# A causal mask of attention scores, added by two 64-row matmuls instead of one of 128 rows

## The chip, the cores and the metric

The kernel runs on one core of a Trainium2 chip. The metric is the device time of one execution in microseconds, as the median of several runs. TensorE is called PE here (PEld is its weight load), VectorE DVE, ScalarE ACT, GpSimd POOL, SyncE SP. All times are in microseconds unless marked ns.

## What is computed

The input x has 16 batches of 256 tokens with 128 features. Four layers follow each other, each with a layer norm in front and a residual behind: causal attention, a mixture of experts (8 experts, the best 2 for each token), a second attention without a mask, and the mixture of experts again. Only the first attention is touched by the change:

```python
B, T, D, H = (4, 256, 128, 16)      # x has 16 batches; HD = 8
q, k, v = proj(wq, bq), proj(wk, bk), proj(wv, bv)
scores = jnp.einsum('bhqd,bhkd->bhqk', q, k) * scale
mask = jnp.triu(jnp.full((t, t), NEG, jnp.float32), k=1)
attn = jax.nn.softmax(scores + mask, axis=-1)
out = jnp.einsum('bhqk,bhkd->bhqd', attn, v)
return out @ wo + bo
```

## The kernel before

Each attention layer is a pipeline over j = 0 to 19. In step j the engines work on several batches at once: the projections of batch j (P_), the values V and the scores S of batch j-2 (V_, S_), the transposed scores T of batch j-3 (T_), the output projection of batch j-4 (O_). Every engine has its own instruction stream, written out by hand (`pe_step`, `act_step`, `dve_step`, `pool_step`, `sp_step`), in which a loop over the 16 heads h carries the other work between the heads. The streams are tied by counting semaphores; `after(engine, semaphore, value)` is a wait.

q and k are split into three bf16 parts each, so that six products stand for one float32 product: 6 × 8 = 48 rows a head (50 for T, which carries minus the row maxima as two more rows). These rows of the even and odd heads stand in SBUF partitions 0 to 47 and 64 to 111 (`qst`, `kst`), so a score matmul uses one half of TensorE's 128 rows. For head h, with par = h % 2:

- S: scores of 128 queries by up to 256 keys, in row half par, in the PSUM bank `psS[par]`. S0 (queries 0 to 127, 128 columns) and S1 (queries 128 to 255, 256 columns) are both line 355. They are only needed for the row maxima.
- T: the transposed scores, in the other row half and the bank `psT[1 - par]`, T0 (256 columns) and T1 (128 columns), line 363. ACT takes their exponential into `pT` (line 553).
- The order of issue is S0, T0, S1, T1, then the mask of T (line 382, only in batches 14 and 15; in the others POOL clears the masked part of `pT`, line 790), then the mask of S (line 386). A mask is one matmul that multiplies the bf16 identity `identb` with a 128x128 triangle of -3e38 (`trib`, for T `tritb`) and adds it to the two diagonal blocks of the bank, 2 × 128 columns, over all 128 rows of the array.

DVE waits for the semaphore S, which the last of S's matmuls raises, and reduces the bank to row maxima (line 671). Before S0 of head h PE waits for the maximum of head h-2, before T0 for the exponential of head h-2. After the 16 heads of a half batch the maxima go through a transpose (line 342), ACT, DVE (line 633) and two DMAs to rows of `qst`.

Between the heads of a full step PE does, behind the mask of the head named: head 1 transposes of the maxima (line 342) and the last quarter of P·V (line 321); head 2 the transposes of x (269); heads 4 and 11 the output transposes (328); head 5 P·V, then the q and k projections (276, four matmuls a batch); heads 6 and 13 a transpose (333), at 13 behind P·V; heads 8 and 14 the output projection (337); head 9 P·V and the maxima (342); head 12 the values (426). Behind heads 0, 3, 7, 10 and 15 nothing stands, and the next head's S0 follows at once. P·V uses 32 weight columns a head and writes 32 output partitions.

DVE has, besides the maxima, the merge of the maxima of two halves (659), the layer norm of the next batch (583), normalising (641, 643), the residual (651), the values with their bias (705), and behind the maxima of heads 11 and 14 the residues of the bf16 split (627).

At the start POOL fills the constants (lines 1750 to 1758) and counts them on `s_const`; DVE waits for 6, after the layer norm of the first two batches, casts the identity to bf16 (line 1791) and permutes the weights (574, 576). PE waits in `pe_setup` for the permuted weights and for `s_const_dve` 2 and then makes the bias columns (line 254).

Of the kernel before, what the change touches and what calls it, by code (L numbers as in the profile page):

```python
# [8 lines left out]
BF16 = mybir.dt.bfloat16  # L9
I32 = mybir.dt.int32  # L10
ALU = mybir.AluOpType
ACT = mybir.ActivationFunctionType
AX_X = mybir.AxisListType.X

P = 128
B, T, D = 16, 256, 128
H, HD = 16, 8
NBLK = B * T // P
TERMS = 6
ROWS = TERMS * HD  # L20
E, HID = 8, 512
HB = HID // P
G = 2
# [8 lines left out]
OWN_A = 2 * (SIZE[0] + PART) + E - 1  # L32
CST_DESC, CST_TILE, CST_HEAD, CST_TRIU = 0, E, E + TILES, E + TILES + P
CST_COLS = CST_TRIU + P
FETCH = 3
EPS = 1e-5
NEG = -3.0e38
# [31 lines left out]
def build(nc, A, out):  # L69
    with ExitStack() as ctx:  # L70
        def sb(name, shape, dt=F32):
            return ctx.enter_context(nc.sbuf_tensor(name, shape, dt))

        def psum(name):
            return ctx.enter_context(nc.psum_tensor(name, [P, 512], F32))

        def sem(name):
            return ctx.enter_context(nc.semaphore(name))
# [5 lines left out]
        psS = [psum("psS0"), psum("psS1")]  # L84
        psT = [psum("psT0"), psum("psT1")]
# [5 lines left out]

        x = sb("x", [P, NBLK, D])
        cst = sb("cst", [P, CST_COLS])
# [2 lines left out]
        nwt = sb("nwt", [P, 3, NBLK])  # L96
        ident = sb("ident", [P, P])
        identb = sb("identb", [P, P], BF16)
        trib = sb("trib", [P, P], BF16)
        tritb = sb("tritb", [P, P], BF16)  # L100
        ones_row = sb("ones_row", [1, T])
# [24 lines left out]
        half = sb("half", [1, 2, H])  # L126
# [63 lines left out]
        s_const = sem("s_const")  # L190
        s_const_dve = sem("s_const_dve")
# [57 lines left out]
        def pe_setup(pe, L):  # L249
            s = L.s  # L250
            pe.wait_ge(s["wp"], 4)
            pe.wait_ge(s_const_dve, 2)
            for o in range(2):
                last = nc.tensor.matmul(psM[:, o:o + 1], L.b_perm[0:1, o, :], ones_row[0:1, 0:1],
                                        start=(o == 0), stop=True, skip_group_check=True)
            last.then_inc(s["bcol_ps"], 1)
# [39 lines left out]
        def pe_step(pe, L, j, c, P_, V_, S_, T_, O_):  # L296
# [38 lines left out]
            def out_project(qb):  # L335
                after(pe, s["onT"], 2 * bO + qb + 1)
                nc.tensor.matmul(psN[:, P:2 * P], onT[:], L.w_in[:, 3, :], start=True, stop=True).then_inc(s["y"], 1)  # L337

            def max_transposes(b, u):
                for qb in range(2):  # L340
                    src = mxu if L.causal else mx3
                    last = nc.tensor.transpose((psM, psN)[u][0:8, qb * P:(qb + 1) * P], src[:, u, qb, :], ident[:])
                last.then_inc(s["mT"], 1)

            for h in range(H):
                par, t = h % 2, h // 2
                r64 = slice(64 * par, 64 * par + ROWS)
                m64 = slice(64 * (1 - par), 64 * (1 - par) + ROWS + 2)
                def scores(half):

                    ps, q_, k_ = psS[par], qst[rS], kst[rS]
                    q0 = slice(half * P, half * P + P)
                    n = P if L.causal and half == 0 else T
                    c0 = (P if L.causal else T) * half
                    return nc.tensor.matmul(ps[:, c0:c0 + n], q_[r64, t, q0], k_[r64, t, 0:n],  # L355
                                            start=(half == 0), stop=True, skip_group_check=True)
# [9 lines left out]
                if S_:  # L366
# [3 lines left out]
                    last_s = scores(0)  # L370
                if T_:
# [3 lines left out]
                    last_t = scores_t(0)  # L375
                if S_:
                    last_s = scores(1)
                if T_:
                    last_t = scores_t(1)
                    if L.causal and bT >= MASKED:  # L380
                        diag = psT[1 - par][:, 0:3 * P].rearrange("p (a k) -> p a k", a=3)[:, 0:3:2, :]
                        last_t = nc.tensor.matmul(diag, identb[:], tritb[:].unsqueeze(1).to_broadcast([P, 2, P]),
                                                  start=False, stop=True, skip_group_check=True)
                    last_t.then_inc(s["ST"], 1)
                if S_ and L.causal:
                    last_s = nc.tensor.matmul(psS[par][:, 0:3 * P].rearrange("p (a k) -> p a k", a=3)[:, 0:3:2, :],  # L386
                                              identb[:], trib[:].unsqueeze(1).to_broadcast([P, 2, P]),
                                              start=False, stop=True, skip_group_check=True)
                if S_:
                    last_s.then_inc(s["S"], 1)  # L390
                if T_ and h in (5, 9, 13):
# [8 lines left out]
                if h == 1 and S_ and not L.causal:  # L400
# [5 lines left out]
                                     start=True, stop=True, skip_group_check=True)  # L406
                    for u in range(2):
                        last = nc.tensor.matmul(psM[0:8, 2 * H + u:2 * H + u + 1],
                                                prow[0:1, 2, 8 * u:8 * u + 8], ones_row[0:1, 0:1],
                                                start=False, stop=True, skip_group_check=True)  # L410
# [159 lines left out]
        def dve_setup(dve, L):  # L570
            s = L.s
            dve.wait_ge(s["w"], 16 * 4)
            for o in range(2):
                nc.vector.tensor_copy(L.w_perm[:, o, :].rearrange("p (a t i) -> p a t i", a=2, t=8),
                                      L.w_in[:, o, :].rearrange("p (t a i) -> p a t i", a=2, t=8)).then_inc(s["wp"], 1)
                nc.vector.tensor_copy(L.b_perm[:, o, :].rearrange("p (a t i) -> p a t i", a=2, t=8),
                                      L.b_in[:, o, :].rearrange("p (t a i) -> p a t i", a=2, t=8)).then_inc(s["wp"], 1)
# [295 lines left out]
        def dve_ln_stats(dve, lo, hi, done):  # L873
            dve_ln_moments(dve, lo, hi)
            dve_ln_root(lo, hi, done)
# [872 lines left out]
        @block.gpsimd  # L1748
        def _(pool):
            nc.gpsimd.memset(ident[:], 0.0).then_inc(s_const, 1)  # L1750
            nc.gpsimd.memset(trib[:], 0.0).then_inc(s_const, 1)
            nc.gpsimd.memset(tritb[:], 0.0).then_inc(s_const, 1)
            pool.wait_ge(s_const, 3)
            nc.gpsimd.affine_select(out=ident[:], in_=ident[:], compare_op=ALU.not_equal, fill=1.0, base=0,
                                    pattern=[[-1, P]], channel_multiplier=1).then_inc(s_const, 1)
            nc.gpsimd.affine_select(out=trib[:], in_=trib[:], compare_op=ALU.is_ge, fill=NEG, base=0,
                                    pattern=[[-1, P]], channel_multiplier=1).then_inc(s_const, 1)
            nc.gpsimd.affine_select(out=tritb[:], in_=tritb[:], compare_op=ALU.is_ge, fill=NEG, base=0,
                                    pattern=[[1, P]], channel_multiplier=-1).then_inc(s_const, 1)
            for r in range(RING):  # L1760
                if r == 0:
                    nc.gpsimd.memset(zero[:], 0.0).then_inc(s_zero, 1)
                ins = nc.gpsimd.memset(kst[r][:].rearrange("p t q -> p (t q)").bitcast(F32), MINUS_ONES)
            pipeline(pool_step, pool, LA)
            pool_ffn(pool, 0)
            pool.wait_ge(s_half, 2)
            pipeline(pool_step, pool, LB, 2)
            pool_ffn(pool, 1)
            for pair in range(2 * PART, 2 * SIZE[1]):
                pool_gather(pool, 3, pair)  # L1770
# [13 lines left out]
        @block.vector  # L1784
        def _(dve):
            nc.vector.memset(ones_row[:], 1.0).then_inc(s_const_dve, 1)
            dve.wait_ge(s_xin, 16)
            dve_ln_stats(dve, 0, 4, s_lnA)
            dve.wait_ge(s_lnA, 1)
            dve.wait_ge(s_const, 6)  # L1790
            nc.vector.tensor_copy(identb[:], ident[:]).then_inc(s_const_dve, 1)
            dve_setup(dve, LA)
            pipeline(dve_step, dve, LA)
            for l in range(2):
                dve.wait_ge(r_sem["slots"], 4 * l + 2)
                tile_loop(dve_tile, dve, l, before=dve_route, behind=dve_behind)
                if l == 0:
                    pipeline(dve_step, dve, LB, 2)
            dve_route_part(dve, 3, 2)
            for q in range(QUADS[1]):  # L1800
                dve_combine_1(dve, 1, q)

        @block.tensor
        def _(pe):
            pe.wait_ge(s_const, 6)
            pe_setup(pe, LA)
            pipeline(pe_step, pe, LA)
            for l in range(2):
                s = (LA, LB)[l].s
                pe.wait_ge(s["exp"], 16 * B)  # L1810
                pe.wait_ge(s["mx"], 16 * B)
                pe.wait_ge(r_sem["slots"], 4 * l + 2)
                pe.wait_ge(LB.s["bcol"], 1)
                tile_loop(pe_tile, pe, l, before=pe_route)
                if l == 0:
                    ffn_over(pe, 0)
                    pipeline(pe_step, pe, LB, 2)
# [40 lines left out]
```

## Time and profile before

| | us |
|---|---|
| timed runs, median | 1162.33 |
| timed runs, lowest to highest | 1160.31 to 1164.01 |
| span of the profiled execution | 1164.9 |

The profiled execution is one by itself and not among the timed ones; its own time is given only as its span from first to last instruction, 1164.9.

| engine | busy us | share |
|---|---|---|
| PE | 1029.9 | 88% |
| PEld | 716.6 | 62% |
| DVE | 755.5 | 65% |
| ACT | 672.4 | 58% |
| POOL | 525.5 | 45% |

The span has four stages in time, one for each layer: causal attention until about 345 us, then the experts, the second attention from about 580 to 910, and the experts again. Busy shares over the whole span mix these stages. A busy time of an engine counts overlapping instructions once; the ends of matmuls are modelled, their starts are not, so distances are best taken from start to start.

### The profile page before, as it was taken

The numbers are of one execution on the slowest core, as the hardware profiler recorded it, in microseconds if no ns is written. First come the engines' busy times: TensorE is split into PE (matmuls) and PEld (weight loads), VectorE is DVE, ScalarE is ACT, GpSimd is POOL, SyncE is SP. The second block draws the span as 40 slices with busy tenths as digits, with TensorE's granted clock in tenths as the row PEclk, the third lists the DMA queues.
The fourth block names the chain that finished last, engine by engine and source line by source line (L and its number), as shares of the span: only waits on it lengthen the run. The fifth ranks groups of instructions, "written<-read, shape, count | busy, mean of one in ns | idle before, by whom it ended". The sixth has DMA issues, their size and how long they took to land.

```text
span 1164.9 us, 28879 instructions
## 1 busy us (share of the span) xinstructions
PE 1029.9 (88%) x9290; PEld 716.6 (62%) x9290; DVE 755.5 (65%) x2322; ACT 672.4 (58%) x1399; POOL 525.5 (45%) x980
## 2 busy tenths in 40 slices
PE   2998999897989999999798979999888799999990
PEld 1444555453468989999443434444443589999990
DVE  4687778877777333456777888888877663334442
ACT  2365676663644545556277858897757445455550
POOL 2243444332742610344687736455736436004455
PEclk9998999996989999999778979998888899999995
DMA  6446544562235878887544323343221469778873
GB/s 152 104 114 138 116 110 99 151 181 57 54 118 174 271 233 236 260 255 236 125 111 104 101 56 85 89 107 84 65 49 44 130 191 280 227 242 256 272 225 109
DMA packets 201723, 175.03 MB, mean 150 GB/s; under 512 B 19812, under 2 KB 160616, under 8 KB 201576
## 3 DMA queue, kind: packets, MB, share of 16 engines
q1 hardware_dynamic: 193384, 156.41, 49.1%
q0 software_dynamic: 8192, 16.79, 4.8%
q8 instruction: 76, 1.25, 0.5%
q14 instruction: 71, 0.58, 0.2%
HBM read 122.99 MB, written 50.14 MB: 149 GB/s over the span
## 4 chain that ended last, share of the span: by engine, by line
PE 60%; DVE 11%; issue 6%; POOL 5%; DMA 4%; SPq 3%; ACT 1%; POOLq 0%; ACTq 0%; DVEq 0%
PE psS L1358 9%; PE psT L1365 9%; PE psO L321 8%; PE psS L355 7%; PE psO L1381 4%; PE psN L1381 4%; DVE mx L671 4%; PE psS L386 3%; PE psT L363 3%; POOL xn L1259 3%; PE psM L276 2%; PE psN L328 2%; DMA eo<-ysb 2%; PE psN L337 1%; PE psM L1346 1%
## 5 line engine op out<-in xcount | busy, mean ns | idle before, releaser
L671 DVE TENSOR_REDUCE mx<-psS 128x3 f32<-128x384 f32 (+1 forms) x512 | 311.4, 617 | 119.5 <-PE psS L386 61.8
L355 PE MATMUL psS<-kst,qst 48*128 48x256 bf16 (+1 forms) x1024 | 201.7, 286 | 46.4 <-DVE mx L671 33.2
L558 ACT ACTIVATE pT<-psT,scb 128x512 f32<-128x512 f32 x256 | 193.9, 777 | 43.2 <-PE psT L363 40.7
L363 PE MATMUL psT<-qst,kst 50*128 50x256 bf16 (+1 forms) x1024 | 194.7, 278 | 4.6 <-DMA qst<-scr_m 2.2
L1422 DVE TENSOR_TENSOR hT<-sg,psT 128x512 f32<-128x512 f32 x142 | 97.5, 686 | 154.4 <-PE psT L1365 127.7
L1245 POOL DMA_INDIRECT xg<-xn,slot x128 | 123.1, 962 | 131.3 <-DVE ysb L1417 72.1
L1358 PE MATMUL psS<-xTt,wgc 128*128 128x128 f32 x1136 | 153.7, 279 | 5.7 <-issue 5.3
L355 PEld LDWEIGHTS psS<-kst,qst 48*128 48x128 bf16 x1024 | 66.2, 97 | 146.0 <-DVE mx L671 68.2
L1365 PE MATMUL psT<-xTt,wuc 128*128 128x128 f32 x1136 | 152.2, 278 | 1.5 <-DMA wuc<-in_L_ffn_Wu 1.4
L790 POOL TENSOR_SCALAR_AFFINE_SELECT pT<-pT 128x256 f32<-128x256 f32 x224 | 90.6, 412 | 133.0 <-ACT pT L553 131.8
L553 ACT ACTIVATE pT<-psT 128x384 f32<-128x384 f32 x256 | 122.9, 490 | 46.1 <-PE psT L363 35.9
L1358 PEld LDWEIGHTS psS<-xTt,wgc 128*128 128x128 f32 x1136 | 140.0, 194 | 9.2 <-issue 8.5
L1365 PEld LDWEIGHTS psT<-xTt,wuc 128*128 128x128 f32 x1136 | 140.0, 194 | 2.3 <-DMA wuc<-in_L_ffn_Wu 2.3
L321 PE MATMUL psO<-pT,vp 128*32 128x256 f32 (+1 forms) x2048 | 141.0, 399 | 0.4 <-ACT pT L558 0.3
L1259 POOL DMA_INDIRECT pT<-eo,slot x64 | 60.4, 944 | 175.9 <-DVE ysb L1417 105.7
L1401 ACT ACTIVATE sg<-psS 128x512 f32<-128x512 f32 x142 | 84.7, 596 | 83.0 <-PE psS L1358 82.9
L1409 ACT ACTIVATE wdc<-wd 128x512 f32 x142 | 89.5, 630 | 52.1 <-issue 48.7
L321 PEld LDWEIGHTS psO<-pT,vp 128*32 128x32 f32 x2048 | 57.6, 118 | 55.5 <-issue 29.1
L1392 ACT ACTIVATE xTt<-psM 128x128 f32<-128x128 f32 x142 | 39.3, 277 | 70.5 <-PE psM L1346 70.3
L386 PE MATMUL psS<-trib,identb 128*128 128x256 bf16 x256 | 77.5, 303 | 0.0
L1381 PE MATMUL psN<-wdc,hT 128*128 128x128 f32 x576 | 76.2, 275 | 1.0 <-DVE ysb L1417 1.0
L1381 PE MATMUL psO<-wdc,hT 128*128 128x128 f32 x560 | 74.3, 276 | 0.5 <-DVE ysb L1417 0.5
(225 smaller groups left out, 1595.1 us busy)
## 6 DMA issues: line engine op xcount, KB each, us to landing
wgc<-in_L_ffn_Wg SPq DMA_DIRECT2D x142, 256.0 KB, 3.1
wuc<-in_L_ffn_Wu SPq DMA_DIRECT2D x142, 256.0 KB
scr_part<-part SPq DMA_DIRECT2D x128, 128.0 KB, 2.1
qst<-scr_part SPq DMA_DIRECT2D x64, 192.0 KB, 3.7
kst<-scr_part SPq DMA_DIRECT2D x64, 192.0 KB, 4.7
xin<-xg SPq DMA_DIRECT2D x142, 64.0 KB
eo<-ysb SPq DMA_DIRECT2D x142, 64.0 KB
scr_part<-part SPq DMA_DIRECT2D x32, 192.0 KB, 1.9
```

The costliest lines, as they stand in the source:

```text
L321: last = nc.tensor.matmul(psO[q // 2][32 * i:32 * i + 32, o0 + dst[0]:o0 + dst[1]], vp[r][:, kb, h, :], pT[:, h % 8, src[0]:src[1]], start ...
L355: return nc.tensor.matmul(ps[:, c0:c0 + n], q_[r64, t, q0], k_[r64, t, 0:n], start=(half == 0), stop=True, skip_group_check=True)
L363: return nc.tensor.matmul(ps[:, c0:c0 + T - q0], k_[m64, t, half * P:half * P + P], q_[m64, t, q0:T], start=(half == 0 or not L.causal), s ...
L386: last_s = nc.tensor.matmul(psS[par][:, 0:3 * P].rearrange("p (a k) -> p a k", a=3)[:, 0:3:2, :], identb[:], trib[:].unsqueeze(1).to_broad ...
L553: nc.scalar.activation(pT[:, g % 8, 0:cols], psT[g % 2][:, 0:cols], ACT.Exp, scale=float(HD) ** -0.5).then_inc(s["exp"], 1)
L558: nc.scalar.activation(pT[:, g % 8, 0:cols], psT[g % 2][:, 0:cols], ACT.Exp, scale=scb[r][:, 0, i:i + 1], bias=scb[r][:, 1, i:i + 1]).then ...
L671: nc.vector.tensor_reduce(mx3[:, u, 0:n, pos:pos + 1].rearrange("p a b -> p (a b)"), psS[h % 2][:, 0:kcols(L)].rearrange("p (a k) -> p a k ...
L1245: nc.gpsimd.indirect_dma_start(xg, bass.IndirectOffsetOnAxis(ap=slot[g][:, i, k:k + 1], axis=0), xn[:, BASE[g] + k, :], None).then_inc(r_s ...
L1358: last = nc.tensor.matmul(psS[p][:, cols], wgc[n % FETCH][:, cols], xTt[n % FETCH][:], start=True, stop=True, skip_group_check=True)
L1365: last = nc.tensor.matmul(psT[p][:, cols], wuc[n % FETCH][:, cols], xTt[n % FETCH][:], start=True, stop=True, skip_group_check=True)
L1381: last = nc.tensor.matmul(psY[p][:, 0:P], hT[(n0 + k - 2) % FETCH][:, hb, :], wdc[(n0 + k - 2) % FETCH][:, hb * P:(hb + 1) * P], start=(hb ...
L1422: nc.vector.tensor_tensor(out=hT[(n0 + k) % FETCH][:].rearrange("p a c -> p (a c)"), in0=sg[p][:], in1=psT[p][:], op=ALU.mult).then_inc(f[ ...
```

## The change

The mask of S and that of T are each made by two matmuls of 64 rows instead of one of 128, both in the row half (group) in which the scores of that bank were made. Half 0 adds the triangle to output rows 0 to 63, half 1 to rows 64 to 127. The weights select the output rows: where the half has the same number as the row group it is `identb`, otherwise the new `identx`, an identity with its column halves swapped. The triangle is kept once for each row group, relative to the group's first row. A half that needs fewer columns gets fewer: for S half 0 has 2 × 128 and half 1 2 × 64 columns, for T the other way round. POOL makes `trib` and `tritb` in two pieces of 64 rows each, with a wait between, DVE makes `identx` by two copies, and the counts that PE and DVE wait for rise.

```diff
+HALF_P = P // 2
...
+        identx = sb("identx", [P, P], BF16)
...
             pe.wait_ge(s["wp"], 4)
-            pe.wait_ge(s_const_dve, 2)
+            pe.wait_ge(s_const_dve, 4)
...
+            def mask_half(bank, group, half, tri, t0, c0, n):
+
+                rows = slice(HALF_P * group, HALF_P * group + HALF_P)
+                select = identb if half == group else identx
+                diag = bank[:, 0:3 * P].rearrange("p (a k) -> p a k", a=3)[:, 0:3:2, c0:c0 + n]
+                return nc.tensor.matmul(diag, select[rows, :],
+                                        tri[rows, t0:t0 + n].unsqueeze(1).to_broadcast([HALF_P, 2, n]),
+                                        start=False, stop=True, skip_group_check=True)
...
                     if L.causal and bT >= MASKED:
-                        diag = psT[1 - par][:, 0:3 * P].rearrange("p (a k) -> p a k", a=3)[:, 0:3:2, :]
-                        last_t = nc.tensor.matmul(diag, identb[:], tritb[:].unsqueeze(1).to_broadcast([P, 2, P]),
-                                                  start=False, stop=True, skip_group_check=True)
+                        last_t = mask_half(psT[1 - par], 1 - par, 0, tritb, HALF_P, 0, HALF_P)
+                        last_t = mask_half(psT[1 - par], 1 - par, 1, tritb, 0, 0, P)
                     last_t.then_inc(s["ST"], 1)
                 if S_ and L.causal:
-                    last_s = nc.tensor.matmul(psS[par][:, 0:3 * P].rearrange("p (a k) -> p a k", a=3)[:, 0:3:2, :],
-                                              identb[:], trib[:].unsqueeze(1).to_broadcast([P, 2, P]),
-                                              start=False, stop=True, skip_group_check=True)
+                    last_s = mask_half(psS[par], par, 0, trib, 0, 0, P)
+                    last_s = mask_half(psS[par], par, 1, trib, 0, HALF_P, HALF_P)
...
-            nc.gpsimd.affine_select(out=trib[:], in_=trib[:], compare_op=ALU.is_ge, fill=NEG, base=0,
-                                    pattern=[[-1, P]], channel_multiplier=1).then_inc(s_const, 1)
-            nc.gpsimd.affine_select(out=tritb[:], in_=tritb[:], compare_op=ALU.is_ge, fill=NEG, base=0,
-                                    pattern=[[1, P]], channel_multiplier=-1).then_inc(s_const, 1)
+            for group in range(2):
+                rows = slice(HALF_P * group, HALF_P * group + HALF_P)
+                pool.wait_ge(s_const, 4 + 2 * group)
+                nc.gpsimd.affine_select(out=trib[rows, :], in_=trib[rows, :], compare_op=ALU.is_ge, fill=NEG, base=0,
+                                        pattern=[[-1, P]], channel_multiplier=1).then_inc(s_const, 1)
+                nc.gpsimd.affine_select(out=tritb[rows, :], in_=tritb[rows, :], compare_op=ALU.is_ge, fill=NEG,
+                                        base=-HALF_P, pattern=[[1, P]], channel_multiplier=-1).then_inc(s_const, 1)
+            pool.wait_ge(s_const, 8)
...
-            dve.wait_ge(s_const, 6)
+            dve.wait_ge(s_const, 8)
             nc.vector.tensor_copy(identb[:], ident[:]).then_inc(s_const_dve, 1)
+            nc.vector.tensor_copy(identx[:, 0:HALF_P], ident[:, HALF_P:P]).then_inc(s_const_dve, 1)
+            nc.vector.tensor_copy(identx[:, HALF_P:P], ident[:, 0:HALF_P]).then_inc(s_const_dve, 1)
...
-            pe.wait_ge(s_const, 6)
+            pe.wait_ge(s_const, 8)
```

## Rows read from the trace of the kernel before

**Rows 1.** The page's first line.
```profile
span 1164.9 us, 28879 instructions
```

**Rows 2.** The chain that ended last, shares by line, from 120 to 310 us.
```profile
by line: PE psO L321 16.2%; PE psS L355 14.9%; PE psS L386 14.5%; DVE mx L671 6.9%; PE psT L363 5.2%; issue 5.0%; PE psM L276 4.5%; PE psN L328 4.0%; PE psN L337 2.2%; PE psN L333 1.9%; PE psM L426 1.9%; PE psO L969 1.8%; DVE part L627 1.7%
```

**Rows 3.** Busy times by stage: PE, PEld, DVE, ACT, POOL, PE's clock, DMA share, GB/s.
```profile
150.00:175.00 25.00, 24.45 (x278) 12.88 (x271) 18.61 (x47) 17.88 (x45) 11.54 (x28) 1.00 0.52 116
...
275.00:300.00 25.00, 21.84 (x184) 10.30 (x184) 19.62 (x67) 10.00 (x23) 10.49 (x20) 0.59 0.30 77
```

**Rows 4.** Timeline of line 276: start, duration; the first and last of six.
```profile
121.80 1.13 PE L276 MATMUL psM<-xT,w_permA 128*128 128x256 f32 x4
...
201.19 1.13 PE L276 MATMUL psM<-xT,w_permA 128*128 128x256 f32 x4
```

**Rows 5.** Timeline of PE, from head 14's mask over heads 15 and 0 to head 1.
```profile
162.35 0.28 PE L386 MATMUL psS<-trib,identb 128*128 128x256 bf16 x1
...
162.99 0.23 PE L355 MATMUL psS<-kst,qst 48*128 48x128 bf16 x1
...
163.05 0.27 PE L355 MATMUL psS<-kst,qst 48*128 48x256 bf16 x1
163.11 0.22 PE L363 MATMUL psT<-qst,kst 50*128 50x128 bf16 x1
163.26 0.28 PE L386 MATMUL psS<-trib,identb 128*128 128x256 bf16 x1
163.47 0.23 PE L355 MATMUL psS<-kst,qst 48*128 48x128 bf16 x1
...
164.50 0.23 PE L355 MATMUL psS<-kst,qst 48*128 48x128 bf16 x1 [0.43 <-DVE mx L671]
```

**Rows 6.** The same view, masks with P·V and with a 128-row transpose behind them.
```profile
168.43 0.28 PE L386 MATMUL psS<-trib,identb 128*128 128x256 bf16 x1
168.65 0.86 PE L321 MATMUL psO<-pT,vp 128*32 128x256 f32 x16
...
170.77 0.28 PE L386 MATMUL psS<-trib,identb 128*128 128x256 bf16 x1
170.89 0.27 PE L333 MATMUL psN<-ident,on 128*128 128x128 f32 x1
```

**Rows 7.** The same view, S0 and S1 of a head in the second attention layer.
```profile
646.10 0.28 PE L355 MATMUL psS<-kst,qst 48*128 48x256 bf16 x1
...
646.22 0.27 PE L355 MATMUL psS<-kst,qst 48*128 48x256 bf16 x1
```

**Rows 8.** Timeline of DVE beside Rows 5.
```profile
162.67 0.56 DVE L671 TENSOR_REDUCE mx<-psS 128x3 f32<-128x384 f32 x1
163.15 0.82 DVE L627 TENSOR_TENSOR part<-rest,part 128x512 bf16<-128x512 f32 x1
163.89 0.55 DVE L671 TENSOR_REDUCE mx<-psS 128x3 f32<-128x384 f32 x1
```

**Rows 9.** Timeline of PE, the two masks of a head in batch 15.
```profile
303.97 0.28 PE L382 MATMUL psT<-tritb,identb 128*128 128x256 bf16 x1
...
304.09 0.27 PE L386 MATMUL psS<-trib,identb 128*128 128x256 bf16 x1
```

**Rows 10.** Timeline of the start, all engines.
```profile
1.77 0.28 POOL L1756 TENSOR_SCALAR_AFFINE_SELECT trib<-trib 128x128 bf16<-128x128 bf16 x1
...
7.72 0.23 DVE L1791 CAST identb<-ident 128x128 bf16<-128x128 f32 x1
7.87 0.22 DVE L574 COPY w_permA<-w_inA 128x128 f32<-128x128 f32 x1
```

**Rows 11.** Timeline of PE and PEld, two weight loads and their second matmul.
```profile
199.91 0.09 PEld L355 LDWEIGHTS psS<-kst,qst 48*128 48x128 bf16 x1 [0.17 <-DVE mx L671]
...
199.93 0.10 PEld L355 LDWEIGHTS psS<-kst,qst 48*128 48x128 bf16 x1
...
199.98 0.27 PE L355 MATMUL psS<-kst,qst 48*128 48x256 bf16 x1
```

## The prediction

> **What bounds the kernel now.** I read the page's head first, then the chain of work that ended last, the busy times by stage, and the timeline of PE and DVE through one batch. The profiled span is 1164.9 us [rows 1]. That is 2.6 us above the median of the three timed runs (1162.33), so I work out differences against the span and add them to the median. Only the first attention layer is causal. In its steady part the chain is mostly TensorE: the masks alone are 14.5% of it, the score matmuls 14.9%, P·V 16.2%, and 6.9% is DVE's maximum [rows 2]. From 150 to 175 us PE is busy 24.45 of 25 us, DVE 18.61, ACT 17.88, POOL 11.54 [rows 3]. The reader should not conclude that PE time saved is time saved: the next question is what one head waits for.
>
> The steady part is very regular. The projection of a batch (four matmuls on line 276, once in 16 heads) starts at 121.80 and, five batches later, at 201.19: 15.88 us each [rows 4]. Within a head, S0 starts at 162.99, S1 at 163.05, T1 at 163.11, the mask at 163.26, the next head's S0 at 163.47 [rows 5]. So the mask starts 0.27 after S0 and the next 64-row matmul 0.21 after the mask; a **direct** head takes 0.48. The two row halves stream side by side: 384 columns of scores in each.
>
> **What a switch between row configurations costs.** A 256-column mask is followed by a 128-row matmul (line 333) after 0.12 us, but by P·V (32-column outputs) only after 0.22 us [rows 6], and by 64-row scores after 0.21 [rows 5]. The difference, 0.09 to 0.10 us, is what changing the shape costs. It is paid again from T1 (128 columns) to the mask: 0.15 us, where 0.06 would be the columns. In the second layer, without mask, 64-row matmuls of 256 columns in one half follow each other in 0.12 [rows 7]. So I price a half mask of 256 columns at 0.12 and one of 128 at 0.065 (S0 to S1: 0.06 to 0.07 [rows 5]), with no switch between scores and masks.
>
> **New head.** Half 0 starts when S1 is through: 0.065 + 0.12 = 0.185 after S0. Half 1 starts at 0.305. Both are in one row half, so they queue: 384 columns instead of 256. What follows decides:
> - Next head's scores, in the other half, can start behind half 1's start: 0.31 to 0.315 instead of 0.48 to 0.49. Saves 0.17. Heads 0, 3, 7, 10, 15.
> - A 128-row matmul (maxima, xT, output transposes, projections, V): the switch is not removed, it moves behind the masks. 0.305 + 0.15 = 0.455 instead of 0.27 + 0.12 = 0.39. Costs **0.065**. Heads 1, 2, 4, 6, 8, 11, 12, 14.
> - P·V: there was a switch on both sides of the mask, now one: 0.305 + 0.15 + 0.01 = about 0.47 instead of 0.49. Saves 0.02. Heads 5, 9, 13.
> - DVE's maximum starts 0.32 after the start of a 256-column mask (162.35 to 162.67 [rows 5, 8]), so 0.27 after half 1's: 0.575 after S0 instead of 0.59.
>
> On PE alone a batch would save 5 × 0.17 + 3 × 0.02 − 8 × 0.065 = 0.39 us of 15.88.
>
> **Where DVE takes it back.** Two score banks: S of head h waits for the maximum of head h−2. Maximum to the next use of its bank is 163.89 to 164.50, 0.61 us [rows 5, 8]. Two heads therefore take at least 0.27 + 0.32 + 0.61 = 1.20 now, and 0.575 + 0.61 = 1.185 afterwards, whatever PE could do. Walk once round, from head 1:
> - Heads 2 and 3 together, 6 and 7 together: already at 1.20. Their direct saving is lost; each pair gains 0.015: −0.03.
> - Heads 1, 4, 8, 11, 12 on PE's path, each +0.065: +0.325.
> - Heads 5, 9, 13: −0.06.
> - Head 10, direct, between P·V with transposes and head 11, where DVE is free: −0.17.
> - Head 14 to head 1 is DVE's: maximum 162.67, residue of the split 163.15, maximum 163.89, head 1 at 164.50 with PE idle before it [rows 5, 8]. The saving of heads 15 and 0 becomes idle time of PE; only the signal of head 14 counts: −0.015.
>
> Sum: **+0.05 us a batch**, about nothing. Some nine batches go this way (six starts stand regularly in [rows 4], the neighbours are close); the others wait for layer-norm work on DVE or for the max rows that come back by DMA, and a mask cannot move them. 9 × 0.05 = +0.45.
>
> Ends. In the last two batches the transposed scores are masked too: mask T 303.97, mask S 0.12 later [rows 9]. Now the two pairs of halves lie in different row halves; in order of issue half 1 of S starts at about 0.38 after S0. Its maximum can start at 0.65 instead of 0.27 + 0.12 + 0.32 = 0.71, and a direct head takes 0.39 instead of 0.27 + 0.12 + 0.21 = 0.60. Half of some twelve such places should survive DVE and ACT: I take −0.4, with 0 and −1.5 as ends.
> Start: DVE makes two more copies of 128x64 before the weights are permuted, ahead of PE's first matmul. The nearest row is the 128x128 cast, 0.15 from its start to the next [rows 10]. I take 0.13 each, +0.26, between 0.2 and 0.3; the first layer's chain carries it. The additional POOL instructions and their wait end long before DVE reaches them at 7.7 us: each selection took 0.28 [rows 10], so the estimate is under 1 us on POOL. POOL's later fills of kst move by as much and have slack until the stacks are loaded. No DMA changes. Total +0.3: 1165.2 for the span, **1162.7** for the median.
>
> **A rule that speaks against the change.** Rows: two weight loads of the same half start 0.02 apart, the second while the first head matmul streams, and the second matmul starts 0.07 after the first [rows 11], though a load lasts 0.1; so loads in one half are largely hidden. The Trainium skill, "TensorE: Matmul & The Clock Gate", Part 3 (The mechanism), says that a weight load overlaps running matmuls only when their row groups differ. The halves share the group of their scores, so by that rule the sum would be rival 2's. The trace speaks against it for loads of scores.
>
> **Rivals.**
> 1. *The halves cost just their columns* (0.107 and 0.053), and a switch 0.09: a 128-row follower loses 0.04 only, P·V saves 0.06, a direct head 0.22, the signal 0.05. The walk gives 5 × 0.04 − 3 × 0.06 − 0.22 − 3 × 0.05 = −0.35, of which DVE's unbroken run from head 11 lets through about 0.23. 9 × 0.23 = 2.1, with the ends at −1.5 + 0.26: about 1159.0. For it: the walk is a difference of small numbers. Against: 0.12 in [rows 7]. 18%, a bit over half of it beyond 0.3%.
> 2. *Weight loads are not hidden in the same half*: two loads of 0.095 behind each other. Each head on the path costs 0.19 more; with 5 + 3 + 1 heads and 3 signals, 12 × 0.19 = 2.3 a batch, 21 us: about 1184. It decides as soon as half 1 starts later than 0.36 after S0. 5%.
> 3. *The halves still drain* (the change doesn't do what it says): half 0 at 0.27, half 1 at 0.39, then 0.15. Followers +0.15 where 128 rows, +0.05 else; signal +0.07: about 5 × 0.15 + 3 × 0.05 + 0.05 + 3 × 0.07 = 1.2 a batch, 11 us: 1173. For it nothing but that no row shows a bank's mask in a row half. 6%.
> 4. *The clock falls.* From 275 to 300 us the granted clock was 0.59, in 150 to 175 it was 1.00 [rows 3]. Afterwards PE waits longer before head 1 in every batch. One more such stretch at 1.2 instead of 2.4 GHz costs the streaming part, by the shapes above about 0.2 a head: 25 heads, 5 us: 1168. 10%.
>
> **How the numbers follow.** The forecast has 61%: 1162.7, its own range 1160 to 1165.5. About 0.3% (3.5 us) is what a measurement can tell from no change. Faster: over half of rival 1 and a tail of the forecast, 16%. Slower: rivals 2 and 3, most of 4, and a tail: 21%. Same: 63%. The range 1158.5 to 1168 takes rival 1 whole and reaches rival 4.
>
> **What would show it.** Half 0 about 0.185 and half 1 about 0.305 behind S0; next S0 0.31 behind at head 0, but a 128-row follower at 0.455 (now 0.39); idle of PE before head 1 near 0.9 us with DVE's maximum as its end; line 276 still near 15.9 apart. A period under 15.6 or above 16.2 makes the walk wrong; a follower at 0.39 makes the price of the moved switch wrong; a changed clock between 120 and 220 us makes rival 4 right.

## The result, and the profile after: 1.2% slower

The changed kernel takes 1177.06 us against 1162.66 in the same set, ratio 1.0123, interval 1.0096 to 1.015. On other occasions, each beside its own runs of before, its ratio was 1.0086 (1.0070 to 1.0103), 1.0072 (1.0038 to 1.0107) and 1.0099 (1.0066 to 1.0132), and with T's masks left alone 1.0095 (1.0069 to 1.0121). The forecast was 1162.7, in 1158.5 to 1168: wrong in size and sign. The profiled execution was the fastest of its four (1172.8), with a span of 1170.8. The ratios are worked out from all the runs of a set and are not quotients of the two medians (1.0072 stands for nine runs between 1164.47 and 1177.32, whose medians alone would give 1.0107). All times and clocks are those of fast runs; one of the six runs of experiment 7 was in a slower state and is left out.

The page of the changed kernel: its first line, busy times, the granted clock in 40 slices.

```profile
span 1170.8 us, 29461 instructions
...
PE 1022.4 (87%) x9578; PEld 736.4 (63%) x9578; DVE 756.0 (65%) x2324; ACT 669.4 (57%) x1399; POOL 527.8 (45%) x982
...
PEclk9998999977889999999769979999888899999995
```

PE is busy less (1022.4 us, before 1029.9) with 288 matmuls more: the two halves overlap with what stands beside them. Here is PE over two heads in the full-speed part, a direct head from 169.39 and one with the output transposes behind it, then one with P·V; it answers to [rows 5, 6].

```profile
169.39 0.23 PE L366 MATMUL psS<-kst,qst 48*128 48x128 bf16 x1
...
169.45 0.27 PE L366 MATMUL psS<-kst,qst 48*128 48x256 bf16 x1
169.51 0.22 PE L374 MATMUL psT<-qst,kst 50*128 50x128 bf16 x1
169.56 0.27 PE L346 MATMUL psS<-trib,identx 64*128 64x256 bf16 x1
169.68 0.21 PE L346 MATMUL psS<-trib,identb 64*128 64x128 bf16 x1
169.74 0.23 PE L366 MATMUL psS<-kst,qst 48*128 48x128 bf16 x1
...
170.18 0.66 PE L330 MATMUL psN<-ident,oT 128*128 128x128 f32 x4
...
170.76 0.23 PE L366 MATMUL psS<-kst,qst 48*128 48x128 bf16 x1
...
171.05 0.21 PE L346 MATMUL psS<-trib,identb 64*128 64x128 bf16 x1
171.20 0.86 PE L323 MATMUL psO<-pT,vp 128*32 128x256 f32 x16
```

The array does what the prediction said: half 0 starts 0.17 behind S0, half 1 0.29, the next scores 0.35 (before 0.48), a 128-row follower 0.44 (before 0.39), P·V 0.44 (before 0.49). P·V is counted from the S0 at 170.76. The regular part is even a little faster, the projection 15.77 us apart in most steps where [rows 4] have 15.88:

```profile
140.44 1.13 PE L278 MATMUL psM<-xT,w_permA 128*128 128x256 f32 x4
...
156.21 1.13 PE L278 MATMUL psM<-xT,w_permA 128*128 128x256 f32 x4
```

So the loss is elsewhere. The distance from one projection to the next tells where (starts of the group on line 276 or 278, from the timelines; "start alone" is the second experiment; the second to fourth profile of the changed kernel are those of experiments 1, 12 and 15):

| | first start | step 5 to 7 | 7 to 12, the usual step | 13 to 15 |
|---|---|---|---|---|
| before | 11.11 | 38.5 | 15.88 | 41.2 |
| start alone | 11.96 | 37.1 | 15.88 | 41.5 |
| changed | 11.95 | 40.1 | 15.77 | 44.2 |
| changed, second profile | 11.96 | 40.3 | 15.77 | 44.1 |
| changed, third | 11.95 | 43.6 | 15.77 | 44.1 |
| changed, fourth | 11.95 | 43.2 | 15.77 | 44.1 |

Against the start alone the steps 5, 6, 13 and 14 lose 5.7 to 9.1 us. Not all of that need be the halves' doing: from 13 to 15 experiment 9, which has no half mask there, takes 43.0 us too, and experiment 11, the start alone again, 41.4. In these steps PE stands: for DVE's layer norm of the second half of the blocks, and for maxima that come back by DMA. In step 5 it looks like this, first the kernel before (T0 of a head waits for the row maxima; then PE waits for DVE), then the changed one:

```profile
86.23 0.28 PE L363 MATMUL psT<-qst,kst 50*128 50x256 bf16 x1 [0.41 <-DMA qst<-scr_m]
...
93.69 0.23 PE L355 MATMUL psS<-kst,qst 48*128 48x128 bf16 x1 [2.67 <-DVE mx L671]
```

```profile
88.62 0.28 PE L374 MATMUL psT<-qst,kst 50*128 50x256 bf16 x1 [1.77 <-DMA qst<-scr_m]
...
97.55 0.23 PE L366 MATMUL psS<-kst,qst 48*128 48x128 bf16 x1 [2.76 <-DVE mx L680]
```

The long wait (2.7 us) is the same in these two profiles. What follows it is not. These are the busy times of the 15 us from that S0 on (columns as in [rows 3], so the third number from the end is the granted clock), for before and for the second profile of the changed kernel:

```profile
93.69:108.69 15.00, 13.87 (x139) 6.87 (x143) 10.88 (x28) 9.46 (x23) 5.58 (x14) 0.86 0.59 161
```

```profile
96.67:111.67 15.00, 14.67 (x138) 8.03 (x138) 9.90 (x26) 8.40 (x21) 4.68 (x11) 0.68 0.57 158
```

A mean of 0.86 is (1 - 0.86) × 2 × 15 = 4.2 us at 1.2 GHz, 0.68 is 9.6 us. PE is as busy, but it gets through fewer of the heads: 26 instructions of DVE instead of 28.

The wait of T0 counts as well. In the changed kernel it took 1.77, 1.51, 1.73 and 1.84 us in the four profiles, and the clock fell behind it: in the 5 us from 88.62 on its mean was 0.66, before it was 1.00 from 86.23 on. In the third profile the clock stayed low from there to the end of the stretch (0.51 from 90.23 to 114.51). This part of the loss thus begins before the long wait; experiment 5 comes back to it.

Do the halves simply cost more at half clock, so that their own path is the loss? Starts in the timelines at 1.2 GHz say no. From S0 to a 128-row follower it is 0.62 us before and 0.75 in the changed kernel (head 14 in step 5: 95.92 to 96.53, and 102.11 to 102.86 in the third profile), from S0 to P·V 0.76 and 0.75, from S0 to the T0 of the head behind a direct one 0.76 and 0.61. Over a whole batch that is 8 × 0.13 − 3 × 0.01 − 5 × 0.15 = +0.3 us, an estimate from these starts. The loss lies in how long the clock stays low.

### The profile page after: what moved, and what is told of

It is laid out like the page before. It is cut to its first block, busy times and chain, and to the rows that moved or that the text cites. A ratio compares the mean times of both kernels' runs of the same rounds, so it can differ in the third digit from the quotient of the medians.

```text
span 1170.8 us, 29461 instructions
## 1 busy us (share of the span) xinstructions
PE 1022.4 (87%) x9578; PEld 736.4 (63%) x9578; DVE 756.0 (65%) x2324; ACT 669.4 (57%) x1399; POOL 527.8 (45%) x982
## 4 chain that ended last, share of the span: by engine, by line
PE 60%; DVE 16%; issue 7%; DMA 6%; POOL 5%; SPq 3%; ACT 2%; POOLq 0%; ACTq 0%; DVEq 0%
PE psS L1367 9%; PE psT L1374 9%; PE psS L366 7%; PE psO L323 7%; DVE mx L680 4%; PE psO L1390 4%; PE psN L1390 4%; PE psM L278 3%; POOL xn L1268 3%; PE psT L374 2%; PE psS L346 2%; PE psN L339 2%; DMA xin<-xg 2%; PE psN L330 2%; PE psM L1355 1%
## 5 line engine op out<-in xcount | busy, mean ns | idle before, releaser
L366 PE MATMUL psS<-kst,qst 48*128 48x256 bf16 (+1 forms) x1024 | 197.3, 288 | 52.0 <-DVE mx L680 38.6
L567 ACT ACTIVATE pT<-psT,scb 128x512 f32<-128x512 f32 x256 | 194.0, 777 | 44.2 <-PE psT L374 41.5
L562 ACT ACTIVATE pT<-psT 128x384 f32<-128x384 f32 x256 | 120.5, 490 | 50.2 <-PE psT L374 40.8
L374 PEld LDWEIGHTS psT<-qst,kst 50*128 50x128 bf16 x1024 | 62.5, 98 | 18.3 <-ACT pT L567 5.2
```

The costliest lines, as they stand in the source:

```text
L374: return nc.tensor.matmul(ps[:, c0:c0 + T - q0], k_[m64, t, half * P:half * P + P], q_[m64, t, q0:T], start=(half == 0 or not L.causal), s ...
L562: nc.scalar.activation(pT[:, g % 8, 0:cols], psT[g % 2][:, 0:cols], ACT.Exp, scale=float(HD) ** -0.5).then_inc(s["exp"], 1)
L567: nc.scalar.activation(pT[:, g % 8, 0:cols], psT[g % 2][:, 0:cols], ACT.Exp, scale=scb[r][:, 0, i:i + 1], bias=scb[r][:, 1, i:i + 1]).then ...
```

## The experiments

"Clock" is the median of the mean granted clock over an experiment's runs; runs of before had 0.921 to 0.922 in every set. Four chips were used, so each is compared with before in its own set.

**1. The changed kernel again.** No edit.

> The changed kernel once more, for a second profile and more timed runs. Clock theory (the batches in the middle are as fast as before, and the loss is time at half clock around waits that the change makes longer): slower than before by 8 to 16 us, the mean granted clock 0.005 to 0.015 under that of before, line 278 still 15.75 to 15.95 apart in its regular part. Path theory (the moved switch costs on PE's path): the same time, but with the clock of before and a period over 16.2. Chance theory (one late DMA in the profiled run): within 6 us of before.

Measured: 1173.11 against 1162.99, clock 0.914, period 15.77. The result is what the clock theory expects; the path theory falls (period not over 16.2), and so does chance.

**2. The start alone.** The changed kernel's start with the masks of before:

```diff
-            for group in range(2):
-                rows = slice(HALF_P * group, HALF_P * group + HALF_P)
...
+            pool.wait_ge(s_const, 4)
+            nc.gpsimd.affine_select(out=trib[:], in_=trib[:], compare_op=ALU.is_ge, fill=NEG, base=0,
...
+            pool.wait_ge(s_const, 6)
+            nc.gpsimd.affine_select(out=trib[:], in_=trib[:], compare_op=ALU.is_ge, fill=NEG, base=0,
...
```

> The start of the changed kernel (POOL's additional selections and waits, DVE's two copies, the higher counts) with the masks of before, 128 rows each. Clock theory by the masks: +0.3 to +1.5 us over before, clock of before. Phase theory (any shift of the start by about 1 us brings DMAs, waits and the clock's falls into another order): +6 us or more, with a clock lower by 0.005 or more.

(Both triangles are selected over 128 rows, and then once more.) Measured: 1165.79, ratio 1.0022 (1.0008 to 1.0035), clock 0.9215; in another set (experiment 11) 1165.69 and 1.0012 (0.9993 to 1.0031), an interval that includes no cost at all. By the medians the start costs 2 to 3 us, more than either of my numbers for it. The first part of it can be seen. The added POOL work pushes the fills of kst behind 3.36 us, and the shifts of DVE's layer norm, 0.17 us each before, run into them. Timeline of the changed kernel's start:

```profile
3.36 2.75 POOL L1776 MEMSET kst<- 128x1024 f32 x3
...
5.27 0.88 DVE L895 TENSOR_SCALAR nwt<-nwt 128x4 int32<-128x4 int32 x1
...
8.60 0.19 DVE L1806 CAST identx<-ident 128x64 bf16<-128x64 f32 x1
8.70 0.22 DVE L583 COPY w_permA<-w_inA 128x128 f32<-128x128 f32 x1
```

The three fills take 0.92 each and end at 6.11; DVE's shift ends at 6.15. Where other experiments delay the fills by one more microsecond, two shifts take 0.88. The copies are 0.10 each from start to start. Experiments 3, 4, 7, 9 and 10 keep two full triangles beside the half ones, which POOL makes too; their first projection starts at 12.73 to 12.75.

**3. Half masks for S alone.** T's masks back to one matmul over 128 rows.

> Half masks for S alone; T of the last two batches is masked over 128 rows as before. If the loss comes from S's masks along the whole layer: within 3 us of the changed kernel. If it comes from the last two batches, where T's halves stand in front of S's: within 4 us of before.

Measured: 1174.62, ratio 1.0095 (1.0069 to 1.0121), clock 0.9165. It is within 3 us of the changed kernel (1173.11): the loss comes from S's masks, not from T's in the last two batches.

**4. Direct heads only.**

```diff
+DIRECT = (0, 3, 7, 10, 15)
+                    if h in DIRECT:
                         last_s = mask_half(psS[par], par, 0, trib, 0, 0, P)
                         last_s = mask_half(psS[par], par, 1, trib, 0, HALF_P, HALF_P)
+                    else:
+                        last_s = nc.tensor.matmul(psS[par][:, 0:3 * P].rearrange("p (a k) -> p a k", a=3)[:, 0:3:2, :],
...
```

> Half masks for S only where the next head's scores follow at once (heads 0, 3, 7, 10, 15), 128-row masks at the eleven others and for T. By the walk of the prediction every 128-row follower is back at 0.39 and only head 10 gains 0.17 a batch: a period of 15.6 to 15.75, 1 to 2 us under the kernel with the start alone. Clock theory: the time beside before is then decided by the half-clock stretches, not by the period; with fewer half masks the clock is between those of before and after, and so is the time (+3 to +10 us).

Measured: 1166.24, ratio 1.0029 (1.0016 to 1.0042), level with the start alone; clock 0.922, period 15.77. Five half masks in sixteen do not lower the clock, where the clock theory expected one between those of before and after. Their period is already the whole 0.11 shorter that the changed kernel has.

**5. Padding.** The start alone, and two waits that are long fulfilled behind each mask, `pe.wait_ge(s_const, 8)`: 576 PE instructions, as many as the change adds.

> The start of the changed kernel, masks of 128 rows, and two waits that are long fulfilled behind each mask on PE: as many more PE instructions as the change has (576), but no more work in the array. Code theory (the longer PE program moves or slows the loading of instructions; SP's fifth copy of the parts in step 5 is issued in 1.8 us instead of 0.7, the max rows come late, PE stands and its clock falls): that issue takes 1.5 us or more, PE waits 1.4 us or more for qst from scr_m there, the steps 5 to 6 of line 276 are 23 us or more apart, the time is 6 to 10 us over the run with the start alone. Shape theory (half masks themselves cost, above all at half clock, because they stream 384 columns in one row half): that issue under 1 us and within 3 us of the run with the start alone.

Measured: 1169.66 against 1165.01, ratio 1.0041 (1.0020 to 1.0062), clock 0.9235, period 16.13. The waits cost 0.25 a batch by themselves, about 8 ns each; the clock does not move, SP's issue took 0.89 and T0 waited 0.51. In the four profiles of the changed kernel that issue took 1.7 to 1.9 us, in experiments 3 and 7 2.2 and 1.9, and there T0 waited 1.5 to 1.9; experiment 10 has the loss with an issue of 0.86 and a wait of 0.80. So the number of PE instructions is not the cause. Why the issue is late stays open, and how much of the changed kernel's time hangs on it is not separated.

**6. One half.** Only the half mask of 256 columns is issued; the masks of S for queries 64 to 127 of each block and of T for keys 0 to 63 are left out.

> Only the 256-column half of each mask is computed, so the rows of the other half stay unmasked: as many PE instructions as before, but in the row half of the scores. Code theory: the issue in step 5 under 1 us, no loss against the run with the start alone (-4 to +1.5 us; a follower of 128 rows should come 0.39 behind S0 as before, a direct head 0.30). Shape theory: part of the loss stays only where a half costs more than the whole mask did; since one half costs less, also -4 to +1.5. What tells them apart is the run with padding.

Measured: 1158.99 against 1165.01, ratio 0.995 (0.9924 to 0.9977), clock 0.914, period 15.15. At the same number of columns and instructions as before the row half is worth 0.73 us a batch; with the clock falling all the same (13.8 of the 15 us behind the layer norm's wait at 1.2 GHz) only 6 us remain of it. The expectation had no fall of the clock in it. The fall needs neither more columns nor more instructions than before.

**7. Followers only**, the complement of experiment 4 (`if h not in DIRECT`).

> Half masks for S only at the eleven heads behind which 128-row work or P.V comes, 128-row masks at heads 0, 3, 7, 10, 15 and for T: the complement of the earlier run. Shape theory: the moved switch is here in full, 11 heads: the time is 7 to 12 us over before, and the regular period is 16.0 to 16.2. Code theory: 352 more PE instructions instead of 576; the loss comes in a jump when the issue in step 5 is late (then 7 to 12 us), otherwise it stays under 4; the regular period 16.0 to 16.2 adds 1 to 2 us at most.

Measured: 1178.36 against 1165.01 (1174.26 to 1191.76), ratio 1.0149 (1.0098 to 1.0201), clock 0.916, period 16.20. The loss is above the 7 to 12 us that were expected, the period 0.32 longer, as expected. That isn't explained by the steps alone: with 0.05 for each of the five followers on PE's path and −0.05 at P·V the prediction's walk gives 5 × 0.05 − 3 × 0.05 = 0.10.

**8. The start mended**, with half masks at the direct heads:

```diff
-            nc.vector.tensor_copy(identx[:, 0:HALF_P], ident[:, HALF_P:P]).then_inc(s_const_dve, 1)
...
+                if l == 0 and j == 1 and h == 0:
+                    nc.vector.tensor_copy(identx[:, 0:HALF_P], ident[:, HALF_P:P]).then_inc(s_const_dve, 1)
...
-            dve.wait_ge(s_const, 12)
+            dve.wait_ge(s_const, 2)
```

On POOL the order is now the identity, then zero and kst, then the triangles.

> Half masks for S at heads 0, 3, 7, 10 and 15 only, with the start mended: POOL fills kst ahead of the triangles, DVE casts only the plain identity ahead of the weights and makes the swapped one later. In the runs before, DVE's shifts in the layer norm waited for POOL's fills (0.88 instead of 0.17 us). If that and the copies are the whole cost of the start, the first projection (line 276) starts at 11.0 to 11.2 again and the time is 0 to 3 us below before (regular period 15.77). If the 3 us of the start alone are something else (code, phase), the time stays 2 to 4 us over before.

Measured: the first projection starts at 11.10 again, 1165.76 against 1165.01, ratio 1.0004 (0.9983 to 1.0025). The collision and the copies are the start's cost up to there; 0 to 3 us below before was not reached.

**9 and 10. Half masks by step**: in steps 3, 4 and 7 to 12 only, and in all other steps only (`j not in REGULAR`). Numbers 11 and 12 are the start alone and the changed kernel in the same set, as measures.

```diff
+REGULAR = (3, 4, 7, 8, 9, 10, 11, 12)
...
+                    if j in REGULAR:
                         last_s = mask_half(psS[par], par, 0, trib, 0, 0, P)
```

> Half masks of S only in the pipeline steps 3, 4 and 7 to 12, in which PE never stands long and the clock stayed at full speed in every profile; 128-row masks in the other steps and for T. Clock theory (half masks cost where the clock has fallen, because it then takes longer to come back): the mean clock is that of the run with the start alone (0.920 to 0.923), the period 15.77, the time 1 us under that run to 1 over it. Path theory (the moved switch costs everywhere alike): half of the loss of the changed kernel, 3 to 5 us over the run with the start alone.

> The complement: half masks of S only in the steps 2, 5, 6 and 13 to 17, in which DVE's layer norm, the DMAs of the maxima or the routing make PE stand. Clock theory: mean clock 0.912 to 0.917, the stretch at half clock behind the layer norm of step 5 over 6 us instead of 3.3, the whole loss of the changed kernel and about 1 us more: 7 to 10 us over the run with the start alone. Path theory: 3 to 5 us over it.

> The run with the start alone again, on the chip of this set, as the measure for the others: 1 to 4 us over before, clock 0.920 to 0.923.

> The changed kernel again, on the chip of this set: 8 to 14 us over before, clock 0.910 to 0.917. With the two runs by steps: clock theory, the loss over the start alone is that of the other steps, within 2 us; path theory, it is the sum of the two in about equal parts.

Measured:

| | median us | clock | ratio to before |
|---|---|---|---|
| 11, start alone | 1165.69 | 0.921 | 1.0012 |
| 9, halves in the regular steps | 1165.56 | 0.922 | 1.0019 |
| 10, halves in the other steps | 1174.23 | 0.916 | 1.0097 |
| 12, changed | 1176.19 | 0.915 | 1.0072 |

This settles where the loss arises. The same half masks cost nothing that can be told in the regular steps and 8.5 us in the others (the interval of 10 is 1.0067 to 1.0127, that of 9 is 0.9994 to 1.0043). The 15 us behind the layer norm's wait in step 5, for experiment 9 and for 10:

```profile
94.73:109.73 15.00, 14.29 (x149) 7.05 (x149) 11.13 (x29) 9.76 (x23) 5.85 (x14) 0.89 0.60 163
```

```profile
95.61:110.61 15.00, 14.67 (x121) 7.84 (x122) 8.72 (x23) 6.90 (x16) 4.29 (x10) 0.55 0.50 147
```

3.3 us at half clock in the one, 13.5 in the other, and 29 against 23 of DVE's instructions. Experiments 2, 4, 9 and 11 all have 0.89 there; the four profiles of the changed kernel 0.77, 0.68, 0.51 and 0.56, number 3 0.54, number 6 0.54. One profile each is not a clean separation: before has 0.86, number 7 has 0.77, and so have 5 and 14, which have no half mask in that stretch; number 8 has 0.67. The verdict rests on the medians and their clocks, in which every kernel with half masks at ten or more heads of the other steps stands at 0.911 to 0.918 and every other at 0.921 or more.

**13. More work behind the wait.** The changed kernel, and in heads 9 to 15 of step 5 and 0 to 8 of step 6 one more matmul over 128 rows, which adds the identity to the diagonal blocks of S:

```diff
+                    if (j == 5 and h >= 9) or (j == 6 and h < 9):
+                        last_s = nc.tensor.matmul(psS[par][:, 0:3 * P].rearrange("p (a k) -> p a k", a=3)[:, 0:3:2, :],
+                                                  identb[:], identb[:].unsqueeze(1).to_broadcast([P, 2, P]),
+                                                  start=False, stop=True, skip_group_check=True)
```

> The changed kernel, and behind S's half masks in heads 9 to 15 of step 5 and 0 to 8 of step 6, the heads that follow the layer norm's wait, one more 128-row matmul of 256 columns, which adds the identity (a shift of a row maximum by at most 1, which softmax takes out). If the clock comes back late because the array has too little to do: the half-clock stretch behind the layer norm's wait shrinks from about 10 us to 3.3 or 6.8, the steps 5 to 6 of line 278 come to 20.5 to 23 us apart instead of 24.3, and the kernel is 1 to 5 us faster than the changed one although it does more. If the halves keep the clock low in another way, or the loss is their path at half clock: the stretch stays at 10 us or more and the time is 2 to 5 us over the changed kernel.

> The changed kernel on the chip of this set, as the measure for the run with additional work: 8 to 14 us over before, clock 0.910 to 0.917.

Measured: 1175.02 (1174.57 to 1178.8) beside 1178.04 (1167.7 to 1179.21) for the changed kernel on the same chip, against 1163.97 for before; clock 0.918 and 0.9115; in the 15 us behind the wait 0.77 and 0.56, so 6.9 us at half clock instead of 13.2. The stretch shrinks as expected and no cost of the additional work can be seen, but the spreads overlap, the ratios (1.0108, and 1.0099 for the changed kernel) are level, and steps 5 to 6 were 25.7 apart (26.5 for the changed kernel), not 20.5 to 23. From 240 to 280 us, where no work was added, the clock differs as much between the two profiles, 0.93 and 0.80. So this experiment doesn't show that the clock comes back late because the array has too little to do; that stays a conjecture.

**14. What is left of the change**: the mended start, half masks in the regular steps only, at heads 0, 3, 5, 7, 9, 10, 13, 15.

> What should be left of the change: half masks for S only in the steps 3, 4 and 7 to 12 and there only behind heads 0, 3, 5, 7, 9, 10, 13 and 15 (direct or with P.V behind), with the mended start. Clock theory: clock of before, period 15.65 to 15.77, time 0 to 2 us below before; with the runs of the mended start and of the regular steps both level with before, no gain that the measurement can tell is as likely.

Measured: period 15.67, clock 0.923, 1164.50 against 1163.97, ratio 1.0019 (0.9997 to 1.0040). No version with complete masks beats the kernel before.

## Why the prediction was wrong, point by point

- **Half 0, half 1, what follows**: right, and each a little cheaper: starts at 0.17 and 0.29 instead of 0.185 and 0.305, a 128-row follower +0.05 instead of +0.065, P·V −0.05 instead of −0.02, a direct head −0.13 instead of −0.17.
- **The walk round a batch**: +0.05 forecast, −0.11 measured, which the cheaper steps give (5 × 0.05 − 3 × 0.05 − 0.13 − 0.05 = −0.08). Experiment 4, with direct heads only, has 15.77 as well. But the walk is not borne out as a whole: for the followers alone it gives +0.10 and experiment 7 measured +0.32, and the two experiments' −0.11 and +0.32 don't add up to the −0.11 of the changed kernel. That the sum comes near is in part luck; the reason is open (a floor set by DVE's path would be one, not tested).
- **The others "wait for layer-norm work on DVE or for the max rows that come back by DMA, and a mask cannot move them"**: this step failed. A mask can't move the wait, but it changes what the clock does after it; experiment 10 puts the loss there with 8.5 us. The wait itself moved too: T0's in step 5 from 0.41 to 1.5 to 1.8 us in the changed kernel.
- **Rival 4, the clock falls**: this is the mechanism as far as the runs show it: the low clocks go with the lost time (0.911 to 0.918 against 0.921 to 0.924). At 10% and 5 us it was undersized, and it was put in a wrong place. I looked for it before head 1 of every batch, where the clock stayed at 1.00 in every profile; it is behind the long waits. Its own condition was in the rows: 0.59 from 275 to 300 us [rows 3] showed that in this layer the clock does fall, and I didn't ask what brings it back.
- **The start**: +0.26 forecast, +0.84 at the first projection and 2 to 3 us in the time. That POOL's fills have slack was true for their readers and false for DVE, which ran into them.
- **The last two batches**: −0.4 forecast; T's masks made no difference that the runs can tell (experiment 3). In [rows 9] the mask of T is that of batch 14 and the mask of S that of batch 15; the two stand side by side in one step only, so there are at most 16 such places.
- **Rivals 1 to 3** (dearer or cheaper halves, loads, drains): the starts in the timeline rule out 2 and 3. S1, half 0 and half 1 start 0.11 to 0.12 apart in one row group, each with its own weights, whose loads take 0.09 to 0.10 by the profile, so the loads are hidden there. The rule of the Trainium skill, "TensorE: Matmul & The Clock Gate", Part 3 (The mechanism), that a load overlaps running matmuls only when their row groups differ, does not hold here.

## What to carry to other kernels

Before you give matmuls a shape that fills less of the array, look where the granted clock is below 1.00 in the kernel as it is. In stretches that run at full speed throughout, price them by starts in the timeline; behind long waits, the clock may stay low longer, as here; leave the full shape there. And a bound that hides PE's savings (here two banks and DVE at 1.2 us for two heads) hides most of them: 0.39 us a batch on PE became 0.11.

## What the runs showed of the hardware

- In the 15 us behind the layer norm's wait PE runs at 1.2 GHz for 3.3 to 4.2 us in four profiles with masks of 128 rows there (before and experiments 2, 9 and 11; wait 2.7 us), but for 6.9 us in two others (5 and 14; wait 2.6 and 2.7), and for 6.9 to 14.7 us (0.77 to 0.51) in the four profiles with all masks in one row half (wait 1.3 to 2.8), though PE is busy 14.4 to 14.7 of these 15 us by its records. The busy time in the profile doesn't show the difference.
- One 64-row matmul in the row half of its neighbours, in place of a 128-row one of the same 256 columns, brings a direct head from 0.48 to 0.18 us and leaves a 128-row follower at 0.37 to 0.38; timeline of experiment 6, S0, half 0, and the next head's S0 and S1:

```profile
156.41 0.23 PE L366 MATMUL psS<-kst,qst 48*128 48x128 bf16 x1
...
156.59 0.27 PE L346 MATMUL psS<-trib,identb 64*128 64x256 bf16 x1
156.59 0.33 PE L366 MATMUL psS<-kst,qst 48*128 48x128 bf16 x2
```

- A DVE shift of 4 integers per partition took 0.88 instead of 0.17 us while POOL filled a 128x1024 float32 tile, and ended 0.04 us behind POOL's fill; two such in a row when the fills came a microsecond later (experiment 3). With the fills done at 4.35 (experiment 8) it took 0.24.
- A fulfilled wait on PE costs about 8 ns, an estimate (0.25 us a batch for 32 of them, experiment 5).
